# Second tile's first half evicted between the score pairs, layout DMAs on ACT's queue, first group turned on TensorE, second layer's weights spread

## The reference

```python
h = jnp.maximum(_layernorm(x, axis=-1), 0.0)
for l in range(2):
    m_left  = jnp.einsum('bsh,oh->bso', h, W_left[l])
    m_right = jnp.einsum('bsh,oh->bso', h, W_right[l])
    u_left  = jnp.einsum('bih,bjh->bij', h, m_left) / temper
    u_right = jnp.einsum('bih,bjh->bij', h, m_right) / temper
    u = u_left * adj_tri + u_left * diag_mask + u_right * jnp.swapaxes(adj_tri, 1, 2)
    e = jnp.exp(u) * adj
    attention = e / (jnp.sum(e, axis=2, keepdims=True) + 1e-10)
    ctx = jnp.matmul(attention, jnp.einsum('bsh,oh->bso', h, W_lin[l]) + b_lin[l])
    h = jax.nn.relu(_layer_norm(ctx, ln_a[l], ln_b[l]))
out = x + h
```

## Time and profile before

| | |
|---|---|
| median of 3 runs | 2853.18 us (2851.03 to 2854.72) |
| the profiled execution's own time | 2853.21 us |
| its span, first to last instruction | 2851.4 us |
| PE busy | 2726.8 us, 96% |
| DVE busy | 1658.9 us, 58% |
| ACT busy | 699.5 us, 25% |
| mean granted clock of PE | 0.994 |

### The profile page before, as it was taken

How to read it: one execution, slowest core, us unless ns; L and a number is a source line. 1 busy time by engine, 2 the same in 40 slices (tenths; PEclk the granted TensorE clock), 3 DMA queues, 4 the chain that set the end, 5 groups by cost and what they waited for, 6 DMA issues and landing times.

```text
span 2851.4 us, 41124 instructions
## 1 busy us (share of the span) xinstructions
PE 2726.8 (96%) x14400; PEld 2453.3 (86%) x14400; DVE 1658.9 (58%) x3394; ACT 699.5 (25%) x1131; POOL 109.2 (4%) x207
## 2 busy tenths in 40 slices
PE   5999999999999999999989999999999999999997
PEld 4888888888888888888878888888888888888886
DVE  5655566555666555655565555565555565555656
ACT  3332222232222222222232222122221122211121
POOL 0000000000000000000000000000000000000000
PEclk9999999999999999999999999999999999999998
DMA  7432223332223332233262222222221222221311
GB/s 171 103 89 82 77 69 78 77 93 82 74 62 79 88 87 80 64 79 89 52 138 51 61 61 57 59 64 58 60 58 50 70 50 61 61 62 54 72 39 57
DMA packets 574473, 207.97 MB, mean 73 GB/s; under 512 B 514272, under 2 KB 532704, under 8 KB 574432
## 3 DMA queue, kind: packets, MB, share of 16 engines
q1 hardware_dynamic: 574432, 207.43, 29.8%
HBM read 125.57 MB, written 77.59 MB: 71 GB/s over the span
## 4 chain that ended last, share of the span: by engine, by line
PE 78%; DVE 8%; SPq 5%; DMA 3%; ACT 3%; issue 2%; ACTq 0%; DVEq 0%
PE pm L580 54%; PE pm L632 14%; PE pu L620 5%; PE pc L649 5%; SPq L370 4%; DVE side L814 3%; DMA ebd<-us 2%; ACT side L709 1%; DVE turned L751 1%; DVE side L818 1%; DVE side L820 1%; DVE et L739 1%; SPq L496 1%; ACT et L716 1%; DMA vec<-in_L_gnn_W_lin_dram 0%
## 5 line engine op out<-in xcount | busy, mean ns | idle before, releaser
L580 PE MATMUL pm<-ht,wt 128*128 128x512 f32 (+1 forms) x7488 | 1616.2, 374 | 39.1 <-DVE ht L739 35.2
L580 PEld LDWEIGHTS pm<-ht,wt 128*128 128x128 f32 x7488 | 1322.4, 189 | 276.7 <-issue 29.2
L632 PE MATMUL pm<-wt,ht 128*128 128x384 f32 x4608 | 828.8, 336 | 50.8 <-DVE hl L739 45.6
L632 PEld LDWEIGHTS pm<-wt,ht 128*128 128x128 f32 x4608 | 800.7, 189 | 61.2 <-DVE hl L739 55.8
L739 DVE TENSOR_TENSOR gt<-pm,gt 128x512 fp32r<-128x512 f32 x384 | 265.2, 691 | 725.7 <-ACT gt L695 724.7
L695 ACT CAST gt<-pm 128x512 fp32r<-128x512 f32 x384 | 224.4, 584 | 1074.0 <-PE pm L580 1073.3
L739 DVE TENSOR_TENSOR hl<-pm,hl 128x384 fp32r<-128x384 f32 x256 | 141.1, 551 | 267.4 <-ACT hl L700 266.4
L700 ACT CAST hl<-pm 128x384 fp32r<-128x384 f32 x256 | 122.2, 477 | 458.5 <-PE pm L632 458.4
L620 PEld LDWEIGHTS pu<-gt,ht 128*128 128x128 f32 x1536 | 210.7, 195 | 9.6
L620 PE MATMUL pu<-gt,ht 128*128 128x256 f32 x1536 | 214.3, 282 | 0.0
L649 PE MATMUL pc<-hl,et 128*128 128x386 f32 (+1 forms) x768 | 160.6, 344 | 20.8 <-DVE et L739 18.8
(11 more groups left out here) (59 smaller groups left out, 726.0 us busy)
## 6 DMA issues: line engine op xcount, KB each, us to landing
rows<-h_dram SPq DMA_DIRECT2D x512, 96.0 KB, 3.0
side<-in_x_dram SPq DMA_DIRECT2D x126, 384.0 KB, 3.4
h_dram<-side SPq DMA_DIRECT2D x126, 384.0 KB, 2.4
out_dram<-side SPq DMA_DIRECT2D x62, 384.0 KB, 2.6
mask<-in_adj_dram SPq DMA_DIRECT2D x32, 128.0 KB, 2.5
ebd<-us SPq DMA_DIRECT2D x64, 64.0 KB, 2.4
side<-in_L_gnn_W_left_dram SPq DMA_DIRECT2D x10, 384.0 KB, 4.0
side<-in_L_gnn_W_right_dram SPq DMA_DIRECT2D x10, 384.0 KB, 4.2
```

The source lines that it names most:

```text
L580: last = nc.tensor.matmul(pm[:, k % M_BANKS, t0 * P:t1 * P], wt[:, lr, a, kc, oc * P:(oc + 1) * P], ht[:, kc, t0:t1, b, :], start=(kc == 0 ...
L632: last = nc.tensor.matmul(pm[:, j % M_BANKS, 0:HALF], ht[:, kc, t, a, :], wt[:, LIN, b, kc, half * HALF:(half + 1) * HALF], start=(n == 0) ...
```

## The change

Four edits.

1. In a group the steps become H00 H01 S5 U0 H10 U1 EX EM EP TX0 T0 H11 adj TX1 H20 T1 ET TX2 H21 C0 H30 T2 TX3 T3 H31 C1. PE's own order is as before. The two layout DMAs of EP are issued by ACT and not by SP.
2. In the first group each normalised tile is transposed by PE in six 128 by 128 blocks into the two `pc` banks, three blocks a bank, and split from there (step P); the store and the loads of that group go away. The M phase's first half (tiles 0 and 1) stands before the last two tiles' steps.
3. The first layer's weights are staged in five slots where there were three.
4. A W step is divided into TW (DVE turns the block) and W (DVE's low part), with other steps between; in group 15 four V blocks lie between the H steps where there were six and one more, and the rest between the M steps. The second layer's staging is still two slots.

```diff
-STAGES = 3
+STAGES = 5
...
-    steps = [("H", 0, 0), *v[0], ("H", 0, 1), ("S", 5), ("U", 0), ("U", 1), ("TX", 0), ("H", 1, 0), ("EX",), ("EM",),
-             ("EP",), ("T", 0), ("H", 1, 1), ("adj",), *v[1], ("TX", 1), ("H", 2, 0), ("T", 1), *v[2], ("ET",),
-             ("TX", 2), ("H", 2, 1), ("C", 0), *v[3], ("H", 3, 0), ("T", 2), ("TX", 3), *v[4], *v[5], ("T", 3),
-             ("H", 3, 1), ("C", 1)]
+    steps = [("H", 0, 0), *v[0], ("H", 0, 1), ("S", 5), ("U", 0), ("H", 1, 0), ("U", 1), ("EX",), ("EM",), ("EP",),
+             ("TX", 0), ("T", 0), ("H", 1, 1), ("adj",), *v[1], ("TX", 1), ("H", 2, 0), ("T", 1), ("ET",), ("TX", 2),
+             *v[2], ("H", 2, 1), ("C", 0), *v[3], ("H", 3, 0), ("T", 2), ("TX", 3), ("T", 3), ("H", 3, 1), ("C", 1)]
...
+    first = [("X", 0, 1), ("X", 1, 1), ("N", 0, 1), ("X", 2, 1), ("N", 1, 1), ("P", 0), sides[0], ("X", 3, 1), ("P", 1)]
+    second = [("N", 2, 1), ("P", 2), ("N", 3, 1), ("P", 3), sides[1], sides[2]]
...
-    change = iteration_steps(True, False, sides[:6], late)
-    change.insert(change.index(("C", 1)), sides[6])
+    late = {0: [sides[4]], 1: [sides[5], *third("t0")], 2: [*third("w0"), sides[6]], 3: third("t1"),
+            4: [*third("w1"), sides[7]], 5: [*third("t2"), sides[8]], 6: [*third("w2 t3"), sides[9]], 7: third("w3"),
+            8: [*third("t4"), sides[10]], 9: [*third("w4 t5"), sides[11]], 10: third("w5")}
+    change = iteration_steps(True, False, sides[:4], late)
...
+                    elif kind == "EP":
+                        act.wait_ge(e_masked, G + 1)
+                        for b in range(2):
+                            own = slice(b * S, (b + 1) * S)
+                            act.dma_start(ebd[b::2, :, own], us[own, :, :]).then_inc(e_moved, 16)
...
+                    if kind == "P":
+                        t = step[1]
+                        pe.wait_ge(x_norm, t + 1)
+                        row = row_slot(0, t)
+                        for half in range(2):
+                            pe.wait_ge(c_clear, 2 * t + half - 1 + C_BANKS)
+                            for j in range(KC // 2):
+                                kc = half * KC // 2 + j
+                                last = nc.tensor.transpose(pc[:, half, j * P:(j + 1) * P], row[:, kc * P:(kc + 1) * P],
+                                                           ident)
+                            last.then_inc(c_full, 1)
```

More of the change, by code:

```diff
@@ L98, in regions, with third @@
     sides = [("V", m, b) for b in range(6) for m in (LEFT, RIGHT)]
[L99 to L103, removed]
+    def third(names):
+        return [("TW" if name[0] == "t" else "W", LIN, int(name[1])) for name in names.split()]
+    first = [("X", 0, 1), ("X", 1, 1), ("N", 0, 1), ("X", 2, 1), ("N", 1, 1), ("P", 0), sides[0], ("X", 3, 1), ("P", 1)]
+    second = [("N", 2, 1), ("P", 2), ("N", 3, 1), ("P", 3), sides[1], sides[2]]
     extra = {k: [sides[k + 3]] for k in range(9)}
     extra[1] = extra[1] + [("A",)]
-    for j in range(6):
-        extra[3 + j] = extra[3 + j] + [lins[j]]
-    parts = [(-1, 0, False, start + m_phase_steps(extra, 2))]
+    for k, more in {3: "t0", 4: "w0", 5: "t1", 6: "w1 t2", 7: "w2 t3", 8: "w3 t4", 9: "w4 t5", 10: "w5"}.items():
+        extra[k] = extra.get(k, []) + third(more)
+    early = m_phase_steps(extra, 2)
+    at = early.index(("M", 0, 2, 4))
+    parts = [(-1, 0, False, first + early[:at] + second + early[at:])]
     half = groups // 2
@@ L207, in gnn_kernel @@
         x_loaded = [sem(f"x_loaded{i}") for i in range(4)]
-        n_stored = [sem(f"n_stored{i}") for i in range(4)]
+        n_stored = [sem(f"n_stored{i}") for i in range(2)]
         h_loaded = [sem(f"h_loaded{i}") for i in range(2)]
         h_turned = sem("h_turned")
+        p_hi = sem("p_hi")
         res_loaded = [sem(f"res_loaded{i}") for i in range(2)]
@@ L264, in ht_tile, with ht_half @@
             return ht[:, :, t, part, :].rearrange("p c (n b) -> p c b n", b=2)
+        def ht_half(t, half, part):
+            own = slice(half * KC // 2, (half + 1) * KC // 2)
+            return ht[:, own, t, part, :].rearrange("p c (n b) -> p c b n", b=2)
         def by_graph(tiles):
-            return tiles.rearrange("p (c b n) -> p c b n", c=KC, b=2)
+            return tiles.rearrange("p (c b n) -> p c b n", b=2, n=S)
         def gt_part(k, part):
@@ L424, in _ @@
                     load_weights(t // 2)
-            load_weights(2)
+            for i in range(2, STAGES):
+                load_weights(i)
             load_adjacency(0, 0)
@@ L455, in walk @@
                                 load_h(h0, X, t - 2)
+                    if kind == "P" and step[1] < 2:
+                        sp.wait_ge(c_full, 2 * step[1] + 2)
+                        load_rows(1, step[1])
                     if kind == "TX":
                         t = step[1]
-                        if t < 2 and first + 1 < PER:
-                            sp.wait_ge(n_stored[row_sem(N, t + 2)], row_count(N, t + 2))
-                            if t == 0 and norms and first >= 0:
+                        if t == 0 and first + 1 < PER:
+                            for i in range(2):
+                                sp.wait_ge(n_stored[i], norm_count(N, 2 + i))
+                            if norms and first >= 0:
@@ L490, in walk @@
                         sp.dma_start(adj_t[N], mask[:, :, ADJ, :]).then_inc(adj_t_stored, 16)
-                    if kind == "EP":
-                        sp.wait_ge(e_masked, G + 1)
-                        for b in range(2):
-                            own = slice(b * S, (b + 1) * S)
-                            sp.dma_start(ebd[b::2, :, own], us[own, :, :]).then_inc(e_moved, 16)
-                    if kind in ("V", "W"):
-                        i = w_index(first, step)
-                        sp.wait_ge(v_split if kind == "V" else w_turned, kind_count(first, step))
+                    if kind in ("V", "TW"):
+                        i = w_index(first, block_of(step))
+                        sp.wait_ge(v_split if kind == "V" else w_turned, kind_count(first, block_of(step)))
                         if next_block(i):
```

118 lines of the change are left out of this document (70 added, 48 removed).

## The result

| | before | after |
|---|---|---|
| median | 2852.11 us (2850.87 to 2854.72) | 2922.89 us (2921.67 to 2924.41) |
| ratio | | 1.0247, 95% interval 1.0229 to 1.0265 |
| span | 2851.4 us | 2921.1 us |
| PE busy | 2726.8 us | 2774.7 us |
| granted clock, mean | 0.994 | 0.974 |

The change makes the kernel 2.5% slower. The forecast of 2906 had the sign, and 53 of the 71 us; the time lies above the end of its range, 2920.

What follows compares the result with a forecast made beforehand. The prediction took PE's work list (busy 2726.8 of 2851.4 us) plus its waits as the bound. Its terms: span 2851.4 + 30 + 30 - 2.6 - 11 + 7 = 2905, with 1.8 around it 2906; range 2867 to 2920.

Steps and rivals of the forecast that it cites:

- walk of a steady group: Steady groups: H21 waits 2.9 us for H11's low part, C0 starts later, each group 1.05 us longer, +30 over 29.
- clock: Steady groups: PE's granted clock falls behind H21's new wait, costing +30 us over 29 groups, bounds 0 and 46.
- group 14: Group 14: EP on ACT ends C0's 3.47 us wait for late `ebd` and the clock's fall there, -2.6 us.
- start: First group: first M block at about 17, H00 of group 0 at about 83.5 instead of 94.44, -11 us.
- layer change: Group 15: 15 us of PE waits plus 3 to 4 of lower clock, 19 against 12.1, +7, between 0 and +12.
- last group: Last group: it has no TX and only EP's queue changes, so 0 us.
- in some 8 of 10 groups: Steady groups: expected share in which PE's clock falls behind H21's 2.9 us wait, each fall costing 1.6 less 0.3 us.
- Rival (a): Steady groups: the new wait at H21 comes but PE's clock does not fall; 2873 us, chance 0.17.
- The 0.25 for a transpose: Start: assumed us per PE transpose of a 128-wide fp32 block, taken in the middle between bounds; 24 of them.
- Rival (b): Steady groups: ACT's issues cost nothing, H21 waits 2.4 us, PE's clock still falls in most; 2890 us, chance 0.13.
- Rival (c): Steady groups: H20's removed wait is not replaced, H11's low part being done by 284.3; 2778 us, chance 0.05.
- twice SP's price: Steady groups: upper case for ACT's DMA issue cost, 1.34 us on SP, making each group 1.6 us longer, +46.

Runs made afterwards that it cites:

- the fillers: The changed kernel with 15 matmuls of 384 columns more before H21 in every group but the last; 2882.72 us, ratio 1.0084.
- the second profile: The changed kernel run and profiled once more with no edit; 2923.99 us, ratio 1.0253 to the kernel before.

## Why the prediction fell short

The order of events was right: H20's wait goes, a longer one comes at H21, the clock falls behind it, C0's wait goes, the start gains, the layer change loses. Sizes were off, and the one most off was the term of the clock. The forecast's own terms:

| term | forecast | measured |
|---|---|---|
| walk of a steady group, 29 x | 1.05, +30 | 1.2, +35 |
| clock, 29 x | 0.8 x 1.3, +30 | 1.4, +40 |
| group 14 | -2.6 | -2.2 |
| start | -11 | -13.6 |
| layer change | +7 | +11.3 |
| last group | 0 | -1.6 |
| sum | +53 | +69.7 |

- **The walk.** Its measure is a group that has the wait and no fall: 87.9 with the fillers, 88.0 in the two groups of the second profile, against 86.7, so 1.2 where the forecast had 1.05. The missing 0.15 to 0.2 come from hand-overs. C0 starts 23.3 behind H00 in those groups, where the forecast had 23.03. In the profile of the result pair 1 begins 12.25 behind H00 for 12.18, TX0 15.73 for 15.63, and T0's cast comes 17.30 behind for 17.08, 0.18 behind the end of ACT's issues. Small, but times 29 it is 5 of the shortfall of 16. The price of the issue itself, 1.34 for two by SP's row, was about right (1.27). H21's wait was to be 2.9 and is 3.07.
- **The clock.** The step that failed is "in some 8 of 10 groups", 29 x 0.8 x 1.3 = +30, which measured +40. The loss per fall was right for most (a group of 89.2 for one of 87.9 or 88.0 without the fall is 1.2 to 1.3), but the share was 31 of 31, and every fifth or sixth fall cost about twice as much (90.5), for which the forecast had nothing. Eight in ten is what the shorter wait of 2.51 gave (25 of 31). Rival (a), in which the clock does not fall, is out.
- **The layer change.** The forecast had 15 us of PE's waits in four places and 3 to 4 of lower clock. The four waits add to 0.75 + 3.43 + 3.58 + 6.98 = 14.7, and the clock took 5.1 (5.84, 5.76 and 6.15 where 4.27 is full speed, and 0.13). These are 19.8, about the 19 forecast. But group 15 also has H21's wait of 3.01 and its fall, since it is built from the same steps: the 29 groups that the steady term counted left it out, and the +7 had no place for it. That is the 4 us: 2.6 as in every group, and some 1.3 more because this fall was one of the long ones (6.13).
- **The start** was 2.6 better: H00 came at 80.85, not 83.5. The first block was forecast at 17 (17.50), the second at 28 to 29 (27.47); what came after it was 1.6 shorter than assumed (53.4 from the second block to H00, for 55.0). The 0.25 for a transpose was right in three tiles of four, and nothing in the trace of before told it: it was a middle between two bounds.
- **The last group** was to stay as it is, and its -1.6 is not the change's doing. It is a fall of the clock that comes in some profiles of one kernel and not in others: in the second profile of the changed kernel it is there, and the last group 50.4 long for 49.4 in the first and 51.0 before.
- **Rival (b)** had the wait at 2.4 with issues for nothing: with EP on SP it is 2.51 and a group 1.9 longer in the second layer (88.6). The mechanism of the issue was weighed rightly. **Rival (c)** needed H11's low part 2.4 sooner. Moving it before EX gave nothing, because `et` took its place; only with `et` before TX1 is the order a gain.
- The range ended at 2920, where the bounds of the single terms (wait +46, clock +46, layer change +12) reached further. It was drawn as if high and low terms would cancel; walk, clock and layer change all came out high, and the start and the last group gave back only 4. The upper bound of the walk was also too low by its own working: with twice SP's price the issues end 1.34 later, and T0's cast, H11 and C0 with them, so a group is 2.4 longer and not 1.6, which is +69 and not +46.

## What to carry over

An eviction moved forward frees one bank; what counts is the last thing in the evicting engine's chain before the next point at which the matmul engine must wait. Moving one step only moves the wait, until everything that this point needs (here EX, EM, `et`, H11 and H20) comes before the work that has slack (TX1, T1). A wait that takes the clock down costs about as much again (1.4 for the clock beside 1.2 for the wait here), so order is worth most where it keeps every wait short. And a group with work of its own is to be walked through the steady steps too.

## What the runs showed of the hardware

- Whether a wait of PE takes the granted clock down is not settled by its length alone. Of 31 groups, 3.07 did in 31 (29 in the second profile), 2.51 in 25, and 1.44 with 0.76 one H block behind it, or 0.54 and 0.50, in none. In the kernel with EP on SP a wait of 1.77 ahead of an M block of group 6 did (16.18 for 14.69), and one of 1.92 at the same place of group 14 did not. The Trainium skill, "TensorE: Matmul & The Clock Gate", section "Why this matters for your kernels", warns of idle gaps between bursts of matmuls, of a length that the 3.07 here just reaches and the 2.51 and 1.77 do not. The falls behind 3.07 agree with it; those behind 2.51 and 1.77, and the two groups with 3.07 and no fall, do not.
- The fall is not equally long either. H21 took 4.97, 4.96, 4.83, 6.13, 5.00, 4.99, 4.96, 4.81, 6.13 in groups 2 to 10 behind waits of 3.07 to 3.08, and the other profiles have the same drift. And in the last group C0's waits of 1.81 and 0.54 brought the clock down before the change, not in the first profile after it, but again in the second (PEclk 0.58 in 2891 to 2895, where the first has 1.00). So that is no effect of the change. The timelines of PE there, first of before, then of after:

```profile
2821.71 1.95 PE L649 MATMUL pc<-hl,et 128*128 128x386 f32 x6 [0.53 <-DVE side L846]
2823.45 7.35 PE L632 MATMUL pm<-wt,ht 128*128 128x384 f32 x36
```

```profile
2892.98 1.30 PE L686 MATMUL pc<-hl,et 128*128 128x386 f32 x6 [0.54 <-DVE side L903]
2894.12 6.41 PE L669 MATMUL pm<-wt,ht 128*128 128x384 f32 x36
```

  This is the 1.6 of the last group. What the drift follows was not found out.
- Six transposes of 128 by 128 fp32 blocks on PE took 1.51 ahead of the first M block, where PE ran slow, but 0.88 at 25.28, and 0.82 at 20.80 in the second profile.
- Two small DMAs issued by ACT occupy it for 1.27, and its next cast starts 0.18 later; SP takes 1.35 for the same two. Neither is counted as busy.
- SP takes 2.69 to issue a third block's four loads, but 6.28 behind the three vector loads, in the kernel before too (6.17). Rows of the changed kernel:

```profile
1498.75 2.69 SPq L393 DMA_DIRECT2D side<-in_L_gnn_W_lin_dram  x4
1512.09 0.49 SPq L413 DMA_DIRECT2D vec<-in_L_gnn_ln_b_dram  x1
1512.63 6.28 SPq L393 DMA_DIRECT2D side<-in_L_gnn_W_lin_dram  x4
1522.00 0.98 DVE L819 STREAM_TRANSPOSE turned<-side 128x768 f32<-128x768 f32 x1 [8.35 <-DMA side<-in_L_gnn_W_lin_dram]
```

That is 9.4 from the first issue to the turning, where the forecast took 5.8 up to the use, and it is in the 6.98 that PE waits at 1525.08. Moving the vector loads behind the last block was not tried.
